# Mamba, convolution, attention and shift blocks on one Trainium2 core: the shift block moved from a common tail into the attention loops

## The chip, the cores and the metric

The kernel runs on one core of one Trainium2 chip. The metric is the device time in microseconds (us) of one execution; lower is better. Engines: TensorE (PE; its weight loads are PEld), VectorE (DVE), ScalarE (ACT), GpSimd (POOL) and SyncE (SP), which only starts DMAs.

## The reference

The input x has 16 images of 64 channels of 32x32 pixels, f32. Four residual blocks follow one another, each on the group-normalized x (32 groups of two channels):

1. x += a small Mamba block (state 2) over 1024 positions per image;
2. x += a 3x3 convolution block with batch norm and a 1x1 convolution;
3. x += attention over the 1024 positions of an image: scores from two 32-channel PReLU projections, values from a 64-channel one, softmax over all positions;
4. x += a shift block. Each channel c has a shift theta[c] = (dy, dx). The image is zero-padded, taken at the whole part ft of the shift and one pixel further, and blended with the fractional part dt:

```python
z1 = xp[:, cidx, y0[:, :, None], x0[:, None, :]]
z2 = xp[:, cidx, y0[:, :, None], x1[:, None, :]]
z3 = xp[:, cidx, y1[:, :, None], x0[:, None, :]]
z4 = xp[:, cidx, y1[:, :, None], x1[:, None, :]]
s = z1 * (1 - dy) * (1 - dx) + z2 * (1 - dy) * dx + z3 * dy * (1 - dx) + z4 * dy * dx
s = s * w_dw[None, :, None, None]
return jnp.einsum('bchw,oc->bohw', s, w_pw)
```

The shifts reach over the whole image, so a channel may see mostly padding.

## The kernel before, in words

X holds all of x in the core's memory: partition = image of the pair (2) x channel (64), then 8 pairs, then L = 1024 pixels; HALF is 512. Work goes pair by pair (p = 0 to 7). The order on each engine is written out by hand, and semaphores join them: `then_inc` at the producer, `wait_ge` at the consumer. An engine runs its own list strictly in order, so a wait holds all that is behind it.

**Blocks 1 and 2** (until about 305 us). The convolution's turns (turn1, L1634) already carry the first pair's attention operands and row products. In this stage DVE and ACT also prepare half of the hat matrices of block 4 (distance L759, hat_abs L1070, hat_relu L1075).

**Block 3, the attention loops** (attend: PE L1751, DVE L723, ACT L1180, POOL's sums L1383). Loop p has 16 slots n, one for each of two images (par) and 8 chunks j of 128 keys. In slot n:

- PE: scores(p, n), two matmuls of 512 queries (L1710); two row products of the next pair (rows, L1688), from which the softmax maxima of loop p+1 come; products (L1723), two matmuls that multiply the exponentials with the values. Extras stand in fixed slots: maxima transposed (max_rows, L1700) after slots 0 and 14, operands of pair p+2 (L1666) in slot 2, sums of pair p-1 (L1743) in slots 5 and 6, values of pair p+1 (L1677) in slots 9 and 10.
- ACT: probs, two exponentials of 128x512 (L1154), which scores of the next slot wait for (two PSUM banks); copies and PReLU parts of operands(p+2), inverse (L1176, L1178) for the softmax sum of p-1.
- DVE: two maxima (L692), which rows of the next slot wait for; operands(p+2), add_first (L721), biased, negative and positive (L670, L678, L684) for the values, scaled and residual (L709, L712) of pair p-1 in slots 7 and 8, end_stats (L456) in slots 9 and 14.
- POOL: normed(p+3) (L1368), low_z(p+2) (L1381), then sums(p): for j = 2 to 7 two adds of 128x1024 (L1391), both operands in SBUF. Four slots hold exponentials, so probs waits for adds of j-4.
- SP: stacked(q), 12 DMAs that build the stacked operands of pair q.

In the last loop (lead=False: no row products, no operands, no values) DVE makes all adds (add, L847), since POOL clears buffers for the hat matrices; block 3 of pair 6 ends in that loop, and the group statistics of pairs 0 to 5 are computed in it (coefs_stat L422, group L1467, coefs_var L431, root L1001, coefs_shift L439).

**Block 4, the common tail.** After loop 7: the sums of pair 7, its residual and statistics; all eight pairs are normalized (normed3), transposed so that image, row, or column lie on the partitions (L1840, 64 transposes, copied out by ACT L1248 and DVE L319), shifted in y and in x by 64 + 64 matmuls with hat matrices, one per channel (shift_y L1850, shift_x L1861, with copies L895 and L1261), transposed back (L1896, copies L327 and L1248), multiplied by the 1x1 weights (pointwise3, L1884), added to X (add3, L906) and stored (L410, L413). The hat matrices hold 1 - |distance| where positive, on a block diagonal of buffers cleared by POOL (L1399, L1402); half of them are placed by SP's DMAs, half by DVE and ACT (L839, L1085) in the tail.

The small steps of the statistics, on which the prediction leans (L422):

```python
link(v.tensor_tensor(SQ[:, lo:hi], mean, mean, ALU.mult))                 # L428
v.tensor_tensor(var, var, SQ[:, lo:hi], ALU.add).then_inc(s["stat_ready"], 1)   # L429
```

Of the kernel before, what the change touches and what calls it, by code (L numbers as in the profile page):

```python
# [23 lines left out]
F32 = mybir.dt.float32  # L24
F32R = mybir.dt.float32r
BF16 = mybir.dt.bfloat16
ACT = mybir.ActivationFunctionType
# [13 lines left out]
EPS = 1e-5  # L41

# [59 lines left out]
def build(nc, x, pack, out):  # L102
    with ExitStack() as ctx:
# [14 lines left out]
        EX = sb("EX", [P, 2 * L])  # L118
        MB = sb("MB", [P, 2, CHUNKS, 2], BF16)
        IB = sb("IB", [P, P], BF16)  # L120
        PS = ctx.enter_context(nc.psum_tensor("PS", [P, 8, HALF], F32))
# [60 lines left out]
        ONE = small(1)  # L182
        PRELU = small(2)
# [45 lines left out]
        def both_stacks(b):  # L229
            k = 4 * ((b + 2) % 3)  # L230
            return R[:, k * L:(k + 4) * L].rearrange("p (k e h n) -> p k e h n", k=2, e=2, h=2)
        G3 = RA
        SLOTS = 4
        PT = [[RB[:, (2 * n + par) * L:(2 * n + par + 1) * L] for par in range(2)] for n in range(SLOTS)]
        SA = [[t[:, par * L:(par + 1) * L] for par in range(2)]
              for t in (RB[:, 8 * L:10 * L], RB[:, 10 * L:12 * L], EX)]
        V = [v.rearrange("p (c m) -> p c m", c=CHUNKS)
             for v in (RA[:, 4, :], RB[:, 12 * L:13 * L], RB[:, 13 * L:14 * L])]
        GB = [RB[:, 14 * L:15 * L], RA[:, 5, :], RA[:, 6, :]]
        OT = [RA[:, 7, 0:HALF], RA[:, 7, HALF:L]]  # L240
        EQ, EF = [[RA[:, i, h * HALF:(h + 1) * HALF] for h in range(2)] for i in (0, 2)]

        ZEARLY = [R[:, i * L:(i + 1) * L] for i in (5, 6)]
        ZLATE = [WS[:, i, :] for i in range(2)]

# [23 lines left out]
        def stacks_in(n):  # L269
# [4 lines left out]
        CG = 16  # L274
        ZEROED = (4, 8, 15, 16)
        D = RB[:, 0:PAIRS * L].rearrange("p (c g) -> p c g", c=C)
        AM = [[v.rearrange("p (c m) -> p c m", c=CG) for v in vs]
              for vs in ([R[:, k * L:(k + 2) * L].bitcast(F32) for k in (4, 6)],
                         [R[:, k * L:(k + 2) * L].bitcast(F32) for k in (8, 10)],
                         [RB[:, k * L:(k + 2) * L] for k in (8, 10)],  # L280
                         [RB[:, k * L:(k + 2) * L] for k in (12, 14)])]
        D1 = [WS[:, 0, i * HALF:(i + 1) * HALF].bitcast(F32) for i in range(2)]
        HAT = [[t.rearrange("p (c y) -> p c y", c=CG)
                for t in (W[:, OFF[w]:OFF[w] + HALF], RB[:, (30 + a) * HALF:(31 + a) * HALF],
                          EX[:, a * HALF:(a + 1) * HALF], EX[:, (2 + a) * HALF:(3 + a) * HALF])]
               for a, w in enumerate(("e12", "bc0"))]
        E = RA.rearrange("p b n -> p (b n)").rearrange("p (x g c) -> p x g c", g=4, c=C)
        S3 = RB[:, 0:PAIRS * L].rearrange("p (b n) -> p b n", b=PAIRS)


# [1685 lines left out]
```

## Time and profile before

| | us |
|---|---|
| median of 3 runs | 698.72 |
| lowest and highest | 695.61, 700.11 |
| span of the profiled execution (first to last record) | 697.9 |
| PE busy | 625.1 (90% of the span) |
| DVE busy | 535.1 (77%) |
| ACT busy | 429.5 (62%) |
| POOL busy | 385.2 (55%) |
| start of loop 7, and from there to the end of the span | 589.86, 108.0 |

The profiled execution has its span as its own time here; it lies 0.8 under the median of the runs. In the rows below a time is us from the span's start; a timeline row gives start, length, engine, line, operation, out<-in with partitions x elements, and x the number of instructions merged; a bracket tells an idle time before it and what ended it. An f32 matmul leaves two records. In the rows of stretches, PEclk is the granted TensorE clock as a share of 2.4 GHz.

### The profile page before, as it was taken

The numbers are of one execution on the slowest core, as the hardware profiler recorded it, in microseconds if no ns is written. First come the engines' busy times: TensorE is split into PE (matmuls) and PEld (weight loads), VectorE is DVE, ScalarE is ACT, GpSimd is POOL, SyncE is SP. The second block draws the span as 40 slices with busy tenths as digits, with TensorE's granted clock in tenths as the row PEclk, the third lists the DMA queues.
The fourth block names the chain that finished last, engine by engine and source line by source line (L and its number), as shares of the span: only waits on it lengthen the run. The fifth ranks groups of instructions, "written<-read, shape, count | busy, mean of one in ns | idle before, by whom it ended". The sixth has DMA issues, their size and how long they took to land.

```text
span 697.9 us, 8622 instructions
## 1 busy us (share of the span) xinstructions
PE 625.1 (90%) x2812; PEld 275.6 (39%) x2812; DVE 535.1 (77%) x857; ACT 429.5 (62%) x737; POOL 385.2 (55%) x243
## 2 busy tenths in 40 slices
PE   3795888888789989999989999999999999986996
PEld 1232332233353332234434444343444444335982
DVE  6996899999934465888858787887878888685547
ACT  2478689899644331235555765748476565787772
POOL 2454788887512140216939779595968979430000
PEclk9997999999999997999989999999999999998999
DMA  9000000000015482404003040300304020200006
GB/s 328 7 0 0 1 0 0 0 0 0 1 45 140 112 199 54 106 1 91 0 1 90 1 91 0 71 21 9 83 0 91 0 31 1 30 1 0 1 1 241
DMA packets 28533, 32.36 MB, mean 46 GB/s; under 512 B 16976, under 2 KB 17104, under 8 KB 28368
## 3 DMA queue, kind: packets, MB, share of 16 engines
q1 hardware_dynamic: 27056, 27.33, 15.3%
q10 hardware_dynamic: 1440, 4.55, 2.7%
q8 instruction: 21, 0.34, 0.2%
q14 instruction: 16, 0.13, 0.1%
HBM read 5.83 MB, written 4.19 MB: 14 GB/s over the span
## 4 chain that ended last, share of the span: by engine, by line
PE 58%; DVE 19%; issue 8%; ACT 7%; POOL 4%; DMA 1%; SPq 1%; DVEq 0%; POOLq 0%; ACTq 0%
PE PS L1723 15%; PE PS L1710 10%; PE PS L1688 9%; PE PS L1599 5%; DVE RB L476 3%; PE PS L1608 2%; PE PS L1677 2%; PE PS L1743 2%; DVE RB L552 2%; DVE PS L544 2%; DVE RB L851 2%; DVE RB L559 1%; PE PS L1850 1%; DVE SM L456 1%; DVE SM L692 1%
## 5 line engine op out<-in xcount | busy, mean ns | idle before, releaser
L692 DVE TENSOR_REDUCE SM<-PS 128x1 f32<-128x512 f32 x256 | 165.0, 683 | 65.3 <-PE PS L1688 64.7
L1154 ACT ACTIVATE RB<-PS 128x512 f32<-128x512 f32 x256 | 138.9, 594 | 88.0 <-PE PS L1710 86.9
L1391 POOL TENSOR_TENSOR RB<-RB 128x1024 f32<-128x1024 f32 x60 | 141.1, 2372 | 7.1 <-DVE RB L721 4.8
L1710 PE MATMUL PS<-R 98*128 98x512 f32 x256 | 95.5, 452 | 1.3 <-ACT RB L1154 1.3
L1688 PE MATMUL PS<-R 96*128 96x512 f32 x256 | 88.7, 418 | 6.9 <-DMA R<-R 3.2
L1723 PE MATMUL PS<-RB 128*64 128x512 f32 x320 | 85.4, 616 | 0.0
L1710 PEld LDWEIGHTS PS<-R 98*128 98x128 f32 x256 | 38.8, 189 | 83.4 <-ACT RB L1154 53.9
L1526 PE MATMUL PS<-RA,W 128*128 (+1 forms) x128 | 63.1, 636 | 8.7 <-DVE RB L552 5.3
L1688 PEld LDWEIGHTS PS<-R 96*128 96x128 f32 x256 | 48.7, 193 | 43.1 <-DVE SM L692 18.9
L1391 POOL TENSOR_TENSOR EX<-EX,RB 128x1024 f32<-128x1024 f32 x24 | 56.5, 2373 | 0.8
L1723 PE MATMUL PS<-RB,RA 128*64 128x512 f32 x192 | 52.7, 627 | 0.0
L1381 POOL TENSOR_TENSOR WS<-RA,WS 128x512 fp32r<-128x512 f32 x12 | 18.7, 1562 | 51.6 <-ACT WS L1129 33.2
L1526 PEld LDWEIGHTS PS<-RA,W 128*128 128x128 f32 x128 | 24.5, 201 | 46.0 <-issue 27.5
L1599 PE MATMUL PS<-RB,WC 128*64 128x512 f32 x168 | 41.7, 613 | 0.9 <-DVE RB L640 0.9
L1091 ACT ACTIVATE RB<-X,SM 64x1024 f32<-64x1024 f32 x15 | 18.5, 1242 | 35.8 <-PE PS L1599 24.4
L552 DVE TENSOR_TENSOR_SCAN RB<-RB,PS 128x512 f32<-128x512 f32 x32 | 38.3, 1237 | 0.6
L1160 ACT ACTIVATE R<-PS 2x512 fp32r<-2x512 f32 x32 | 17.2, 582 | 27.7 <-PE PS L1700 27.7
L456 DVE BATCH_NORM_STATS2 SM<-X 128x6 f32<-128x512 f32 x48 | 31.7, 683 | 1.1 <-DMA X<-x 0.8
L476 DVE SCALAR_TENSOR_TENSOR RB<-PS,W,RB 128x1023 f32<-128x1023 f32 (+2 forms) x24 | 30.6, 1280 | 1.5 <-ACT RB L931 0.8
L1321 POOL TENSOR_TENSOR RB<-RB 128x512 f32<-128x512 f32 x16 | 20.3, 1268 | 16.1 <-ACT RB L978 16.0
L1330 POOL TENSOR_TENSOR EX<-RB 128x512 f32<-128x512 f32 x15 | 19.1, 1277 | 17.8 <-DVE RB L564 17.8
L1723 PEld LDWEIGHTS PS<-RB 128*64 128x64 f32 x320 | 16.2, 135 | 30.6 <-issue 26.5
(186 smaller groups left out, 1111.7 us busy)
## 6 DMA issues: line engine op xcount, KB each, us to landing
R<-WS SPq DMA_DIRECT2D x72, 128.0 KB, 2.4
X<-x SPq DMA_DIRECT2D x8, 512.0 KB, 7.4
RB<-RB SPq DMA_DIRECT2D x32, 128.0 KB, 4.0
RB<-RB ACTq DMA_DIRECT2D x14, 280.5 KB, 4.1
out<-X SPq DMA_DIRECT2D x7, 512.0 KB, 2.7
R<-R SPq DMA_DIRECT2D x20, 128.0 KB, 2.4
W<-pack SPq DMA_DIRECT2D x1, 1072.0 KB, 11.6
R<-R ACTq DMA_DIRECT2D x4, 128.0 KB, 3.3
```

The source lines that it names most:

```text
L456: return v.bn_stats(BST[:, p, h, :], half(X, p, h))
L476: i = v.scalar_tensor_tensor(AC[b][:, j:L], xp[:, 0:L - j], col("cw%d" % (3 - j)), AC[b][:, j:L], ALU.mult, ALU.add)
L552: i = v.tensor_tensor_scan(tB[h][j], tA[h][j], bank(1 + j), first, ALU.mult, ALU.add)
L692: v.tensor_reduce(MX[:, par, tile, h:h + 1], bank(2 + h), AX.X, ALU.max)\
L1154: act(slot[:, h * HALF:(h + 1) * HALF], bank(4 + h), ACT.Exp).then_inc(s["p_ready"], 1)
L1321: link(g.tensor_tensor(tM[h], tM[h], tU[h], ALU.add))
L1391: i = g.tensor_tensor(out, out, PT[j % SLOTS][par], ALU.add)
L1526: i = mm(bank(1 + 2 * o + j), mat("bc%d" % (2 * o + j)), half(XS, p, h))
L1599: i = mm(conv_out(k, h), WC[:, 3 * k + dx, :], u[:, y, dx:dx + WW], start=(k == 0 and dx == 0), stop=(k == 1 and dx == 2))
L1688: mm(bank(2 + h), stack(b, par, 0)[0:96, tile * P:(tile + 1) * P], stack(b, par, 1)[0:96, h * HALF:(h + 1) * HALF]).then_inc(s["s_mm"], 1)
L1710: mm(bank(4 + h), stack(b, par, 1)[0:98, j * P:(j + 1) * P], stack(b, par, 0)[0:98, h * HALF:(h + 1) * HALF]).then_inc(s["t_mm"], 1)
L1723: i = mm(PS[par * C:(par + 1) * C, h, :], V[b][:, j, par * C:(par + 1) * C], PT[j % SLOTS][par][:, h * HALF:(h + 1) * HALF], start=(j == 0 ...
```

## The change

Block 4 is no longer a tail over all pairs. Each pair's block 4 is done in the loops that follow its attention: statistics and normalization of pair p-1 in loop p, then a copy in device memory, shifted windows read back from it, blends and the 1x1 matmul in loop p+1 and p+2. There are no hat matrices, transposes and shift matmuls.

- norm3(q) (ACT) writes the normalized pair into PADDED, 32 rows with a pitch of 65, of which 32 are data. spread_out(q) (SP) writes PADDED, 1.06 MB, into one of two scratch tensors in device memory, whose pads were zeroed at the start.
- windows(q) (POOL) issues two indirect DMAs. Each takes, for each of 128 partitions, one run of 1073 elements from the scratch at an offset that depends on the channel's whole shift: 16 output rows and one more. The second takes the lower half of the image, for the other image of the pair, so that halves lie in swapped partitions.
- rows_part and cols_part (ACT) multiply by 1 - fraction, rows_blended and cols_blended (DVE) add the neighbour times the fraction, rows first, then columns; 33 rows of 33 or 32 elements.
- pointwise3 (PE), four matmuls of 64x64 weights, add3 (DVE), store (SP).
- places() and theta() (DVE) compute offsets and fractions in the convolution, in place of distance and the hat operations.
- In the attention itself the values' PReLU is done by ACT (v_parts, two operations a half) and DVE (mixed, one), not by DVE alone; operands, sums, values, high_z, inverse, scaled and residual stand one slot later; SA and V have two buffers, not three.
- In loop 7 the adds are split: DVE adds image 0, POOL image 1, and POOL issues windows(5), windows(6) and windows(7) between.

The diff, cut to its core:

```diff
@@ sync
+            sp.wait_ge(s["zero_set"], 1)
+            for t, of in zip(spread, blocks):
+                sp.dma_start(t[0:LEAD].rearrange("(p n) -> p n", p=16), R[0:16, 0:LEAD // 16].bitcast(F32))\
+                    .then_inc(s["pads_in"], 16)
+                sp.dma_start(of[:, HH * PITCH:BLOCK], R[:, 0:FAR * PITCH].bitcast(F32)).then_inc(s["pads_in"], 16)
+            def spread_out(q, parts=1):
+                need(sp, s["windows_in"], 32 * (q - 1))
+                for h in range(parts):
+                    sp.wait_ge(s["g3_dve" if h else "g3_done"], 1 if h else q + 1)
+                    r = slice(h * HH * PITCH // parts, (h + 1) * HH * PITCH // parts)
+                    sp.dma_start(blocks[q % 2][:, r], PADDED[:, r]).then_inc(s["g3_out"], 16)
...
+            for p in range(1, PAIRS - 1):
+                if p >= 3:
+                    store(p - 3)
+                if p + 2 < PAIRS:
+                    stacked(p + 2, (p + 2) % 3)
+                spread_out(p - 1)
+            store(4)
+            spread_out(6)
+            store(5)
+            spread_out(7, 2)
+            store(6)
@@ vector, attend
+                        if n == 0 and p >= 3:
+                            cols_blended(p - 3)
+                        if n == 2 and p >= 3:
+                            add3(p - 3, 6)
+                        if n in (4, 6) and p + 2 < PAIRS:
                             operands(p + 2, n // 5)
                         if n in (v0 + 1, v0 + 2):
                             biased(p + 1, n - v0 - 1)
+                        if n in (v0 + 2, v0 + 3):
+                            mixed(p + 1, (p + 1) % 2, n - v0 - 2)
...
+                        if n in (8, 9):
+                            scaled(p - 1, n - 8)
+                            residual(p - 1, n - 8)
+                        if n == 10:
+                            end_stats(p - 1, 0)
+                            link(end_stats(p - 1, 1))
+                            coefs_stat(p - 1, p)
+                        if n == 11:
+                            coefs_var(GN3 + p - 1, p - 1, p)
+                        if n == 13:
+                            coefs_shift(GN3 + p - 1, p - 1, p)
+                        if n == 14 and p >= 2:
+                            rows_blended(p - 2)
@@ vector, loop 7 and the end
+            cols_blended(4)
+            add3(4, 2)
...
+            coefs_stat(q, q + 1)
+            add(2)
+            coefs_var(GN3 + q, q, q + 1)
+            rows_blended(5)
+            add(3)
+            coefs_shift(GN3 + q, q, q + 1)
+            add(4)
+            cols_blended(5)
+            add(5)
+            add(6)
+            add3(5, 2)
+            add(7)
...
+            norm3(q, 1)
+            rows_blended(6)
+            cols_blended(6)
+            add3(6, 2)
+            for h in range(2):
+                rows_blended(q, h)
+                cols_blended(q, h)
+            add3(q, 4)
@@ scalar
+            def v_parts(q, b, c):
+                a.wait_ge(s["asm_done"], 2 * q + c + 1)
+                act(v_chunks(b, c), bank(6 + c), ACT.Identity, scale=col("aa")).then_inc(s["v_linear"], 1)
+                act(bank(6 + c), bank(6 + c), ACT.Relu).then_inc(s["v_relu"], 1)
+            def rows_part(q, h=None):
+                k = rows_of(h)
+                a.wait_ge(s["windows_in"], 32 * (q + 1))
+                need(a, s["cols_done"], 2 * q)
+                act(BLENDS[:, k], WINDOWS[:, k, 0:WIDE], ACT.Copy, scale=REST[:, 0:1])\
+                    .then_inc(s["rows_act"], 2 if h is None else 1)
...
+                    if n in (v0 + 1, v0 + 2) and lead:
+                        v_parts(p + 1, (p + 1) % 2, n - v0 - 1)
+                    if lag and lead:
+                        if n == 9 and p >= 2:
+                            rows_part(p - 2)
+                        if n == 12:
+                            root(GN3 + p - 1, p - 1, p)
+                        if n == 14:
+                            norm3(p - 1)
+                        if n == 15 and p >= 2:
+                            cols_part(p - 2)
@@ gpsimd
+            def windows(q):
+                if q == 0:
+                    g.wait_ge(s["pads_in"], 16 * 4)
+                    g.wait_ge(s["places_done"], 1)
+                g.wait_ge(s["g3_out"], 16 * (q + 1) + (16 if q == PAIRS - 1 else 0))
+                need(g, s["pw_mm"], 2 * q)
+                table = spread[q % 2].unsqueeze(1)
+                for h in range(2):
+                    at = bass.IndirectOffsetOnAxis(ap=PLACES[:, h:h + 1], axis=0)
+                    g.indirect_dma_start(SEEN[:, h * WINDOW:h * WINDOW + WINDOW - WW], None, table, at)\
+                        .then_inc(s["windows_in"], 16)
...
+                if p >= 2:
+                    windows(p - 2)
...
+                sums(p)
+            p = PAIRS - 1
+            windows(p - 2)
+            g.wait_ge(s["first_added"], 2 * PAIRS)
+            for j in range(2, 6):
+                add(p, j, 1, True)
+            windows(p - 1)
+            for j in range(6, CHUNKS):
+                add(p, j, 1, True)
+            windows(p)
@@ tensor
     def operands_free(q):
                     t.wait_ge(s["m_copied"], 4 * q - 4)
+                    need(t, s["res_done"], 2 * q - 8)
...
+                    if n == 1 and p >= 3:
+                        if lead:
+                            t.wait_ge(s["m_copied"], 4 * p + 4)
+                            pointwise3(p - 3, 6)
+                        else:
+                            t.wait_ge(s["s_read"], 32 * PAIRS)
+                            pointwise3(p - 3, 2)
...
+                    v0 = 8 if first else 10
+                    if n == v0 and lag and lead:
+                        t.wait_ge(s["x2_done"], 2 * p)
+                        group(GN3 + p - 1, p - 1, p)
                     if n in (v0, v0 + 1) and lead:
+                        if lag and n > v0:
+                            t.wait_ge(s["var_ready"], GN3 + p)
                         values(p + 1, (b + 1) % 3, n - v0)
```

## Rows read from the trace of the kernel before

**Rows 1.** Busy time by stretch: stretch, length, busy us of each engine, PEclk, DMA, GB/s
```profile
500.00:550.00 50.00, 50.00 (x220) 21.49 (x220) 42.31 (x75) 31.62 (x59) 41.01 (x19) 1.00 0.14 32
```

**Rows 2.** Timeline of PE: a slot of loop 5, what follows it, the starts of loops 6 and 7
```profile
510.57 0.74 PE L1710 MATMUL PS<-R 98*128 98x512 f32 x2
...
511.71 1.08 PE L1723 MATMUL PS<-RB 128*64 128x512 f32 x4
...
512.72 0.61 PE L1700 MATMUL PS<-IB,MB 128*2 128x128 bf16 x8
...
550.70 0.74 PE L1710 MATMUL PS<-R 98*128 98x512 f32 x2
...
589.86 0.73 PE L1710 MATMUL PS<-R 98*128 98x512 f32 x2
```

**Rows 3.** Timeline of PE in loop 7 and the tail: group(), next scores, pointwise3, next entry
```profile
595.62 0.39 PE L1472 MATMUL PS<-SM,W 128*128 128x12 f32 x2
...
595.86 0.70 PE L1710 MATMUL PS<-R 98*128 98x512 f32 x2
...
680.62 1.09 PE L1884 MATMUL PS<-RB,W 64*64 64x512 f32 x8 [0.31 <-DVE RB L327]
...
681.64 1.09 PE L1896 MATMUL PS<-W,RA 128*128 128x128 f32 x8
```

**Rows 4.** Timeline of DVE, loop 5: add_first, maxima, scaled, end_stats
```profile
522.88 1.21 DVE L721 TENSOR_TENSOR EX<-RB 128x1024 f32<-128x1024 f32 x1
...
529.82 1.29 DVE L692 TENSOR_REDUCE SM<-PS 128x1 f32<-128x512 f32 x2 [1.17 <-PE PS L1688]
...
531.02 0.69 DVE L709 TENSOR_TENSOR PS<-PS,RA 128x512 f32<-128x512 f32 x1
...
536.08 0.68 DVE L456 BATCH_NORM_STATS2 SM<-X 128x6 f32<-128x512 f32 x1
```

**Rows 5.** Timelines of DVE and POOL: the statistics' small steps, two adds, the steps undisturbed
```profile
591.20 1.10 DVE L428 TENSOR_TENSOR SM<-SM 128x6 f32<-128x6 f32 x1
...
592.34 2.30 DVE L429 TENSOR_TENSOR SM<-SM 128x6 f32<-128x6 f32 x1
...
589.91 4.71 POOL L1391 TENSOR_TENSOR RB<-RB 128x1024 f32<-128x1024 f32 x2 [0.31 <-ACT RB L1154]
...
632.17 0.16 DVE L429 TENSOR_TENSOR SM<-SM 128x2 f32<-128x2 f32 x1
```

**Rows 6.** Timeline of POOL in loop 5: the adds behind low_z
```profile
528.54 16.75 POOL L1391 TENSOR_TENSOR EX<-EX,RB 128x1024 f32<-128x1024 f32 x7
```

**Rows 7.** Timeline of ACT: a pair of exponentials, root, normed3 of 1024 columns
```profile
529.34 1.09 ACT L1154 ACTIVATE RB<-PS 128x512 f32<-128x512 f32 x2 [0.65 <-PE PS L1710]
...
634.34 0.21 ACT L1005 ACTIVATE SM<-SM 128x2 f32<-128x2 f32 x1
...
635.54 1.20 ACT L1235 ACTIVATE RA<-X,SM 128x1024 f32<-128x1024 f32 x1
```

**Rows 8.** Timeline of PE and stretches in the convolution: a wait and the clock around it
```profile
259.80 1.22 PE L1688 MATMUL PS<-R 96*128 96x512 f32 x2 [3.17 <-DMA R<-R]
...
250.00:256.00 6.00, 6.00 (x36) 2.78 (x36) 4.02 (x6) 1.98 (x2) 4.69 (x4) 1.00 0.86 210
...
259.80:262.00 2.20, 2.20 (x10) 0.80 (x10) 1.29 (x2) 0.00 (x0) 0.00 (x0) 0.50 1.01 220
```

**Rows 9.** Timelines of PE and DVE in the tail: sums of pair 7, last add3
```profile
624.97 1.94 PE L1743 MATMUL PS<-RB,W 128*64 128x512 f32 x8 [1.85 <-DVE RB L851]
...
689.53 5.01 DVE L906 TENSOR_TENSOR X<-PS,X 128x512 f32<-128x512 f32 x8 [0.16 <-PE PS L1884]
```

**Rows 10.** DMA issues of the page (KB, us to landing), and SP's last two stores
```profile
X<-x SPq DMA_DIRECT2D x8, 512.0 KB, 7.4
...
out<-X SPq DMA_DIRECT2D x7, 512.0 KB, 2.7
...
693.97 1.11 SPq L413 DMA_DIRECT2D out<-X  x2
```

More of the change, by code:

```diff
@@ L182, in build @@
         ONE = small(1)
+        OMAA = small(1)
+        THETA = small(2)
+        WHOLE = small(2)
+        ABOVE = small(2)
+        FRAC = small(2)
+        REST = small(2)
+        OFFSET = small(1)
+        OFFSETX = small(1)
+        START = small(1)
         PRELU = small(2)
@@ L787, in _ @@
                 biased(0, c)
-                negative(0, 0, c)
-                positive(0, 0, c)
-            at = 0
+            for c in range(2):
+                mixed(0, 0, c)
             for p in (5, 6, 7):
@@ L1219, in _ @@
                     low_stacked()
+                    for c in range(2):
+                        v_parts(0, 0, c)
             max_rows(0, 0, 0)
@@ L1232, in _ @@
-            attend(PAIRS - 1, 1, lead=False, extra=late)
-            def normed3(p):
-                act(G3[:, p, :], X[:, p, :], ACT.Identity, scale=SC[:, p:p + 1], bias=SH[:, p:p + 1])\
-                    .then_inc(s["g3_act"], 1)
-            a.wait_ge(s["coef_ready"], GN3A + 1)
-            for p in range(2, PAIRS - 2):
-                normed3(p)
+            q = PAIRS - 2
+            attend(PAIRS - 1, 1, lead=False,
+                   extra={6: lambda: inverse(q, 0), 7: lambda: inverse(q, 1), 8: lambda: rows_part(5),
+                          10: lambda: root(GN3 + q, q, q + 1), 11: lambda: cols_part(5), 13: lambda: norm3(q)})
@@ L1241, in _ @@
+            q = PAIRS - 1
             for h in range(2):
[L1242 removed]
+                product_out(q, h)
             for h in range(2):
[L1244 to L1258 removed]
@@ L1272, in _ @@
+            root(GN3 + q, q, PAIRS)
+            norm3(q, 0)
+            rows_part(6)
+            cols_part(6)
+            for h in range(2):
+                rows_part(q, h)
+            for h in range(2):
+                cols_part(q, h)
         @block.gpsimd
@@ L1359, in g1 @@
                     .then_inc(s["g1_ready"], 1)
-            for p in range(5):
+            for p in range(3):
+                g1(p)
+            g.memset(PADDED[:, :], 0.0).then_inc(s["pads_set"], 1)
+            for p in (3, 4):
                 g1(p)
@@ L1903, in _ @@
-            t.wait_ge(s["bk_act"], 8)
-            t.wait_ge(s["bk_dve"], 8)
-            for p in range(4, PAIRS):
-                pointwise3(p)
+                sums(PAIRS - 1, h)
+            t.wait_ge(s["x2_done"], 2 * PAIRS)
+            group(GN3 + PAIRS - 1, PAIRS - 1, PAIRS)
+            t.wait_ge(s["res_done"], 2 * 5 + 2)
+            pointwise3(6, 2)
+            t.wait_ge(s["p_ready"], 32 * PAIRS)
+            pointwise3(7, 4)
 def _packed(w):
```

510 lines of the change are left out of this document (176 added, 334 removed).

## The prediction

> **What bounds the kernel now.** I read the busy time by stretch first: from 500 to 550 us PE is busy all 50 us, DVE 42, POOL 41 and ACT 32 [rows 1]. The attention loops are bound by PE. The timeline of PE says how: one slot n of a loop is scores and two row products, 1.14 us until products() begins, and products(), 1.01 until the next entry, so 2.15 us [rows 2]. Sixteen slots and the extras (maxima, z operands, sums, values) give the period: loop 6 starts at 550.70, loop 5 started at 510.57, so 40.1 us; loop 7 starts at 589.86 [rows 2]. From there to the span's end at 697.9 lie 108.0 us: loop 7 and the tail, where all pairs are transposed, shifted by hat matrices and turned back.
>
> So the question has two halves: what the new work adds to loops 1 to 6, where each us of PE or of PE's waiting is paid, and what is left after 589.86. I write T10 for the start of slot 10, and so on.
>
> **Part 1, PE work added to the loops.** pointwise3 is four matmuls in four quadrants, 1.02 us to the next entry [rows 3], in loops 3 to 6: 4.1. group() is 0.25 [rows 3], in loops 1 to 6: 1.5. Moving operands, sums and values by a slot costs PE nothing.
>
> **Part 2, the wait at group().** PE meets group() in slot 10, at T10 + 2.15, and it waits for stat_ready. DVE makes that in its own slot 10, behind the two maxima of slot 10. A maximum pair begins 1.02 after its slot and takes 1.20, scaled with residual 1.35 per half, two end_stats 1.25 [rows 4, 2]. From T8: maxima until +2.2, scaled and residual until +3.6, maxima until +4.8, scaled and residual until +6.1, maxima until +7.3, end_stats until +8.6, bn_aggr until +8.8. T10 is +4.3, so DVE reaches the two tiny tensor_tensors at T10 + 4.55. Undisturbed they take 0.16 each [rows 5], and PE would wait 3.0.
>
> They are disturbed. Both read two SBUF operands, and POOL is in its adds. At the end of loop 6 the same two lines took 1.10 and 2.30, and they end at 592.30 and 594.64, where POOL's two adds, which start at 589.91 and take 4.71, end too [rows 5]. So the first waits for the add that runs, and the second for the whole next add (2.37, [rows 6]). In loops 1 to 5 POOL begins its adds after low_z: high_z moves from slot 5 to slot 6, so 2.15 later than T5 + 5.7 (528.54, [rows 6]), at T5 + 8.0, that is with j=3's second add still running when DVE arrives at T5 + 17.0. I price the rest of that add at 0.4, the whole next one at 2.37: the wait is 3.0 + 0.1 + 0.4 + 2.4 = 5.9. Its bounds are 3.0 and 3.0 + 2.4 + 2.4 = 7.8. In loop 6, without low_z, the adds start earlier and POOL runs dry after the fourth j: 4.45. The Trainium skill, page "SBUF — State Buffer", section on who interferes with whom, says that a VectorE instruction with two SBUF inputs and a GpSimd instruction that reads SBUF exclude each other for a whole instruction. By that rule the wait is the 5.9; by the undisturbed rows it would be 3.0, and that is the second case below.
>
> **Part 3, waits behind it.** In slot 11 values(1) waits for var_ready: maxima until T11 + 2.2, biased (0.7, as scaled) until 2.9, three small ops of 0.2 and a step to PE make 3.6 against 2.15: 1.45. In slot 12 ACT's v_parts waits for biased (T12 + 2.95), takes 1.3, root takes 0.46 [rows 7], and only then comes the exp of slot 13 (half of 1.09, [rows 7]), which scores of slot 14 needs: ready at T12 + 5.4 and 5.9 against 4.3: 1.35 with its second half. At the loop's end coefs_shift (two SBUF operands) and rows_blended meet adds of POOL again, up to 2.37 each; ACT's norm3 stands behind the first, in front of the copies of maxima and the last exps. Walked through, the next loop's scores and rows come 1.8 late (0.9 in loop 1, which has no rows_blended). cols_blended (1.3, as an add of 1024 columns, 1.21, [rows 4]) is blocked until an add ends, and pointwise3 waits for it: 0.8 in loops 3 to 6. operands_free waits for res_done: maxima of slot 2 and two add3 end at T2 + 3.6, PE is there at 2.75: 0.9 in loops 3 to 5. Bounds of this whole part: 0, if DVE and ACT were ahead, and twice my sum, as an add blocks each time fully.
>
> Per loop: p=1: 5.9 + 0.25 + 1.45 + 1.35 + 0.9 = 9.85. p=2: 10.75. p=3, 4, 5: 10.75 + 1.0 + 0.8 + 0.9 = 13.45 each. p=6: 4.45 + 0.25 + 1.45 + 1.35 + 1.8 + 1.8 = 11.1. Together 72.0.
>
> **The clock.** After a wait of 3.17 us at 259.80 PE ran at 0.50 of its clock, the 1.2 GHz level, against 1.00, the 2.4 GHz level, before [rows 8]; eight matmuls took twice as long. A wait of 5.9 in each loop can do that. The slow stretch then lies over slots 11 to 13, where PE waits anyway (1.45 and 1.35), so most is absorbed: 0.5 a loop, 3.0 in all (bounds 0 and 4 a loop).
>
> **Part 4, loop 7 and the tail, from T0 = 0.** POOL's window issue and its wait are new rows. Before, DVE made all adds of loop 7 and the sums stood at 624.97, 35.1 after 589.86 [rows 9, 2]. Now half of them are POOL's, and ACT carries probs (1.09 a slot), inverse (1.2 a half), rows_part, cols_part and norm3 (1.23 for 1024 columns, [rows 7]). Walked through: a slot of PE is 1.7 without row products; pointwise3(4) adds 1.0; probs(3) ends at 8.1; sums(6) stand at 9.7 and 12.2; inverse ends at 13.4 and 15.9, rows_part(5) at 18.3; DVE's residual(6) at 17.3, its statistics at 19.9 (POOL waits for probs then, so one add at most is in the way); group at 20.8, root at 22.4; rows_blended(5) is held by an add and ends at 24.9, so cols_part(5) at 26.2 and probs(11) at 27.3; coefs_shift is held until 28.5, and norm3(6) ends at 29.9. spread_out(6) writes 1.06 MB; a store of 512 KB lands in 2.7 [rows 10], so two in a row would take 5.4; I take 4.3 and 0.7 to issue: 35. POOL stands in windows(6) for it, with adds j=6 and 7 behind: two issues at 0.9 (SP's are 0.56; upper bound a whole landing, 7.4, [rows 10]), then 4.75 for adds: sums at 42.1 with the steps between. From the sums to coef_ready it was 10.0 (624.97, [rows 9]; root ended at 634.8, [rows 7], and coefs_shift follows), of which root stood 0.7 behind copies: 9.3, so 51.4. norm3(7): 52.0. Meanwhile pair 6 is blended (four steps of 1.3 and pointwise3, to 58.4), and windows(7) needs pw_mm of pair 6, so spread_out(7), there at 57, is hidden. windows(7): 1.8 to issue, 2.7 to land (bounds 2.7 and 7.4, [rows 10]): 63. Blends by halves: rows, rows, columns, columns, across ACT and DVE, 5.1; pointwise3 1.0, add3 1.4, with steps 70.7. From the last DVE op (689.53 + 5.01) to the end 3.4 [rows 9]: 74.1, against 108.0. The Trainium skill, page "DMA: Bandwidth & Descriptors", section on the anatomy of one DMA, gives some 2.0 us plus bytes over 436 GB/s for a DMA issued by GpSimd, 3.3 for 549 KB (an estimate from it): with it the tail would be 0.6 longer. No row here shows such a DMA.
>
> **What goes or is hidden.** Removed are 64 + 64 transposes, 128 shift matmuls, their copies and POOL's clears: all in the 108.0. In the convolution ACT loses eight hat operations, DVE four distances and gains some 20 small ones; PE is the bound there; 0, bounds -3 and +4. The pads are written long before their use. In loops 2 to 6 windows() stands before low_z, where POOL waits for high_z; that hides it until an issue costs over 4 us.
>
> **Sum.** 589.9 + 72.0 + 3.0 + 74.1 = 739.0 of span; the span before, 697.9, is 0.8 under the median of its runs, 698.7, so 740.
>
> **Rivals.**
> B, *the adds don't meet the statistics*: PE waits 3.0 at group, the clock stays, the loop boundary is smooth: 740 - 16 (5 x 2.9 and 1.45) - 3 (clock) - 8 (the boundary's 9.9 but 1.9) = 713. For it: a shift of half a us decides on which add DVE falls. Against: [rows 5], the same lines.
> C, *the waits of PE vanish*: DVE has 8 us free in 50, and if the statistics come before PE asks, only PE's work is added: 589.9 + 5.6 + 74.1 + 0.8 = 670, faster. It decides where PE waits less than (108.0 - 74.1 - 5.6) / 6 = 4.7 us a loop. Against: slot 10 stands in both queues, and 2.2 of the wait remain with DVE on time.
> D, *the indirect DMAs are dear*: at 5 us of POOL for each, four stand on the tail's path: 740 + 4 x 4.1 = 756. Nothing in the trace speaks for or against.
> E, *it doesn't do what it says*: windows move in 4-byte pieces, 128 x 1073 of them twice a pair, 275,000: far above 1000.
>
> **Chances.** A 0.5, B 0.2, C 0.05, D 0.15, E 0.02; 0.08 lies between B and C, about no change. Predicted 740; the range takes in B and D with their bounds: 704 to 764. This kernel's measurement tells about 1% from no change. Faster by over 1% (under 691.7): 0.06; within: 0.08; slower: 0.86.
>
> **What would show it.** Right: PE waits for the two-operand statistics line once a loop, some 6 us; loops 3 to 5 last 53 to 54; the granted clock dips after it; tensor_tensor of 128x1 shows over 1 us; from loop 7 to the end some 75. Wrong: loops of 42 to 46 (C), or of 47 to 50 with those lines at 0.16 (B); POOL's issue over 3 us (D).

## The result, and the profile after

The changed kernel takes 730.2 us (median of 4 runs, 729.7 to 732.5) against 697.7 for the kernel before, run beside it: ratio 1.046, interval 1.042 to 1.050. Predicted were 740 with a range of 704 to 764. The direction held, and so did the ground of it, that PE waits in the loops for more than the tail gives back. The largest single term, the wait at group(), came out at half its size. The total was 10 us too high, and two errors of opposite sign hide in that: the loops came out 14.5 us shorter than forecast, the tail 6 us longer. (The profiled execution is the slowest of the four, 2.3 us over their median.)

The page of the changed kernel, busy time of the engines, and then its busy time by stretch in the same 50 us as [rows 1]:

```profile
span 730.6 us, 7908 instructions
...
PE 606.2 (83%) x2440; PEld 240.0 (33%) x2440; DVE 540.0 (74%) x854; ACT 422.1 (58%) x734; POOL 399.1 (55%) x250
```

```profile
500.00:550.00 50.00, 44.19 (x174) 18.30 (x173) 37.93 (x60) 30.62 (x56) 32.48 (x17) 0.93 0.30 86
```

PE was busy all 50 us and is now busy 44, at 0.93 of its clock: the loops aren't bound by PE any more. No other engine has taken over as a whole (DVE 38, POOL 32); what bounds them is a chain that passes back and forth. Who PE waits for stands in its waits in loops 1 to 6 (line waited at, releaser, total, times, longest):

```profile
PE PS L1501 <- DVE SM L451: 18.5, 6, 3.6
PE PS L1740 <- ACT RB L1197: 5.0, 11, 0.7
PE PS L1785 <- DVE RB L749: 2.8, 4, 0.7
PE PS L1718 <- DVE X L756: 2.6, 3, 0.9
...
PE PS L1707 <- DVE SM L458: 1.4, 3, 0.8
```

L1501 is group(), waiting for the statistics; L1740 are the scores, which wait for exponentials; L1785 is pointwise3, behind cols_blended; L1718 is the row product behind operands_free. L1707 are the second values, which wait for var_ready. All five are waits that the prediction named, but not in its sizes: the largest is 3.0 a loop, not 5.9, and the second values wait 1.4 in six loops together, not 1.45 in each. PE's timeline of slots 10 and 11 of loop 3 shows it, and what it does to the clock:

```profile
475.17 1.08 PE L1753 MATMUL PS<-RB,W 128*64 128x512 f32 x4
479.23 0.35 PE L1501 MATMUL PS<-SM,W 128*128 128x2 f32 x2 [2.98 <-DVE SM L451]
479.44 1.14 PE L1707 MATMUL PS<-W,RA 128*128 128x128 f32 x8
480.33 1.00 PE L1740 MATMUL PS<-R 98*128 98x512 f32 x2
481.13 1.05 PE L1718 MATMUL PS<-R 96*128 96x512 f32 x2
482.12 1.98 PE L1753 MATMUL PS<-RB,W 128*64 128x512 f32 x4
```

The same products() take 1.08 ahead of the wait and 1.98 behind it: 2.4 GHz, then 1.2. DVE in that time, and POOL's run of adds:

```profile
478.59 0.29 DVE L450 TENSOR_TENSOR SM<-SM 128x1 f32<-128x1 f32 x1
478.92 0.16 DVE L451 TENSOR_TENSOR SM<-SM 128x1 f32<-128x1 f32 x1
...
491.22 1.83 DVE L466 SCALAR_TENSOR_TENSOR SM<-SM 128x1 f32<-128x1 f32 x1
...
494.28 2.23 DVE L742 SCALAR_TENSOR_TENSOR RA<-RB,SM,RA 128x1089 f32<-128x1089 f32 x1
...
499.51 3.00 DVE L749 SCALAR_TENSOR_TENSOR RB<-RA,SM,RB 128x1056 f32<-128x1056 f32 x1
```

```profile
469.39 19.02 POOL L1423 TENSOR_TENSOR RB<-RB 128x1024 f32<-128x1024 f32 x8
```

The two small statistics steps of [rows 5], there 1.10 and 2.30, are nearly free here (L450, L451). But coefs_shift (L466) on one element takes 1.83, and the two blends (L742, L749) 2.23 and 3.00. The adds did meet DVE: not at group(), but at the loop's end, where Part 3 of the prediction has them too.

The starts of slot 0 (by the maxima product of each loop) give loops 1 to 6 as 52.9, 49.3, 50.9, 52.2, 51.6 and 49.6 us, against 45.4, then 40.1 four times and 38.7: 62.0 us more in all. (Two other profiles with the same instructions in these loops, experiments 8 and 9, have 304.8 and 302.7 us in place of 306.6, so this sum is good to some 4 us.) The scores of loop 7 start at 650.39 ([rows 2]: 589.86), and 80.2 us follow, against 108.0. PE, POOL and ACT in the tail:

```profile
692.58 3.42 PE L1773 MATMUL PS<-RB,W 128*64 128x512 f32 x8 [2.43 <-POOL RB L1423]
700.91 0.56 PE L1501 MATMUL PS<-SM,W 128*128 128x2 f32 x2 [4.91 <-DVE SM L451]
708.99 1.98 PE L1785 MATMUL PS<-RB,W 64*64 64x512 f32 x8 [7.52 <-DVE RB L749]
724.81 1.99 PE L1785 MATMUL PS<-RB,W 64*64 64x512 f32 x8 [13.83 <-DVE RB L749]
```

```profile
711.81 0.95 POOL L1438 DMA_INDIRECT RB<-spread,PLACES  x1 [19.28 <-PE PS L1785]
713.07 0.94 POOL L1438 DMA_INDIRECT RB<-spread,PLACES  x1 [0.30 <-issue]
...
719.36 1.38 ACT L1151 ACTIVATE RA<-RB,SM 128x528 f32<-128x528 f32 x2 [11.94 <-DMA RB<-spread,PLACES]
```

The sums of pair 7 stand behind POOL's last adds (start 42.2 after loop 7's start; predicted 42.1), then POOL stands idle 19.28 us until the pointwise product of pair 6 lets it issue the windows of pair 7. ACT stands idle 11.94 us until these have landed; 7.55 of them lie behind the first issue.

### The profile page after: what moved, and what is told of

It reads as the page before. It is cut to its first block, busy times and chain, and to the rows that moved or that the text cites. A ratio compares the mean times of both kernels' runs of the same rounds, so it can differ in the third digit from the quotient of the medians.

```text
span 730.6 us, 7908 instructions
## 1 busy us (share of the span) xinstructions
PE 606.2 (83%) x2440; PEld 240.0 (33%) x2440; DVE 540.0 (74%) x854; ACT 422.1 (58%) x734; POOL 399.1 (55%) x250
## 4 chain that ended last, share of the span: by engine, by line
DVE 37%; PE 34%; issue 11%; POOL 6%; ACT 6%; DMA 3%; SPq 1%; DVEq 0%; POOLq 0%; ACTq 0%
DVE SM L707 10%; PE PS L1740 5%; PE PS L1718 5%; PE PS L1753 4%; PE PS L1628 4%; DVE RB L498 3%; PE PS L1707 3%; POOL RB L1423 3%; DVE SM L478 2%; PE PS L1637 2%; DVE RB L749 2%; PE PS L1773 2%; DVE RB L575 2%; DVE SM L466 2%; DVE PS L567 2%
## 5 line engine op out<-in xcount | busy, mean ns | idle before, releaser
L1423 POOL TENSOR_TENSOR RB<-RB 128x1024 f32<-128x1024 f32 x90 | 213.7, 2393 | 52.3 <-ACT RB L1197 43.5
L1740 PE MATMUL PS<-R 98*128 98x512 f32 x256 | 101.3, 468 | 8.1 <-ACT RB L1197 7.9
L1718 PE MATMUL PS<-R 96*128 96x512 f32 x256 | 94.6, 435 | 10.3 <-DVE X L756 2.6
L1740 PEld LDWEIGHTS PS<-R 98*128 98x128 f32 x256 | 41.2, 194 | 95.2 <-ACT RB L1197 65.1
L1753 PE MATMUL PS<-RB,RA 128*64 128x512 f32 x256 | 71.8, 641 | 0.0
L1753 PE MATMUL PS<-RB,W 128*64 128x512 f32 x256 | 71.2, 641 | 0.0
L1718 PEld LDWEIGHTS PS<-R 96*128 96x128 f32 x256 | 49.6, 197 | 52.3 <-DVE SM L707 24.9
L1418 POOL TENSOR_TENSOR WS<-RA,WS 128x512 fp32r<-128x512 f32 x12 | 15.3, 1276 | 65.9 <-ACT WS L1138 54.0
L1501 PE MATMUL PS<-SM,W 128*128 128x2 f32 (+3 forms) x28 | 6.4, 300 | 35.1 <-DVE SM L451 34.6
L1438 POOL DMA_INDIRECT RB<-spread,PLACES x16 | 15.5, 970 | 35.0 <-PE PS L1785 27.6
L1785 PE MATMUL PS<-RB,W 64*64 64x512 f32 x64 | 10.5, 729 | 24.1 <-DVE RB L749 24.1
```

What stands on the lines that cost most here:

```text
L1423: i = g.tensor_tensor(SA[p % 2][par], SA[p % 2][par], PT[j % SLOTS][par], ALU.add)
L1718: mm(bank(2 + h), stack(b, par, 0)[0:96, tile * P:(tile + 1) * P], stack(b, par, 1)[0:96, h * HALF:(h + 1) * HALF]).then_inc(s["s_mm"], 1)
L1740: mm(bank(4 + h), stack(b, par, 1)[0:98, j * P:(j + 1) * P], stack(b, par, 0)[0:98, h * HALF:(h + 1) * HALF]).then_inc(s["t_mm"], 1)
L1753: i = mm(PS[par * C:(par + 1) * C, h, :], V[p % 2][:, j, par * C:(par + 1) * C], PT[j % SLOTS][par][:, h * HALF:(h + 1) * HALF], start=(j ...
```

## The experiments

Line numbers in an experiment's rows are its own; the operations are named beside them. Unless it says otherwise, an edit is to the changed kernel, and it is printed without the parts that only carry it ("..."). T1 and T2 are the theories of each expectation. The expectations name a run by a label: e4 and e5 are experiments 4 and 5, e6 is 8, e8 and e10 stand in 10. The medians of the kernel before, run beside each experiment, lie between 697.0 and 699.8, so totals from different experiments compare to some 3 us. The same stretches, loops 1 to 6 in sum, serve for all: 244.6 us before, 306.6 after the change.

**1. group() without its wait.**

```
 def group(nth, lo=0, hi=PAIRS):
+    if GN3 <= nth < GN3 + PAIRS - 2:
+        mm(PS[:, 7, 0:2], mat("pairs"), FIXED).then_inc(s["group_mm"], 1)
+        return
     t.wait_ge(s["stat_ready"], nth + 1)
```

> In loops 1 to 6 the group product reads two constants and no longer waits for the statistics (they are still made). Its result in those loops is that of the constants, so the per-pair coefficients differ. Theory T1 (the 3.0 us wait at the group product sits in TensorE's path and nothing is behind it but a shorter wait at the second part of the values): each loop loses 3.0 us of wait and some 0.3 us of half clock, while about 1.2 us of wait stays at the second values; loops 49.3 to 52.9 become 46 to 49.5, total 708 to 713 us. Rival T2 (VectorE bounds the stretch, so the wait only moves): the second values wait 4 us or more in its place and the total stays above 724 us.

Measured: 708.7 us, loops 287.3, 19.3 less. PE's waits in these loops:

```profile
PE PS L1712 <- DVE SM L459: 12.1, 6, 2.5
```

The wait at the second values is now 2.0 a loop, more than the 1.2 of the expectation. T1 holds: the wait, with the half clock behind it, is worth 3.2 us a loop, although part of it comes back one slot later.

**2. GpSimd busy, but not reading.**

The three memsets stand in for the add in loops 1 to 6 alone:

```
-    i = g.tensor_tensor(SA[p % 2][par], SA[p % 2][par], PT[j % SLOTS][par], ALU.add)
+    link(g.memset(SA[p % 2][par], 1.0))
+    link(g.memset(SA[p % 2][par], 1.0))
+    i = g.memset(SA[p % 2][par][:, 0:128], 1.0)
```

> In loops 1 to 6 each of GpSimd's adds of probabilities is three memsets of about the same time in all (the sums of probabilities are then constants): GpSimd is as busy and signals as late, but reads nothing from SBUF. Theory T1 (GpSimd's two-operand adds hold up VectorE's instructions with two SBUF operands): the coefs_shift step falls from 1.83 to under 0.3 us, the rows blend from 2.23 to about 1.35, the cols blend from 3.00 to about 1.35, and the loops get 1 to 2.5 us shorter each: 715 to 724 us. Rival T2 (it is GpSimd being busy, or its writes): durations and total as they are, 728 to 732 us. The group wait stays at 3.0 us in both.

Measured: 716.5 us, loops 291.8, 14.8 less. DVE's timeline at the end of loop 3 (coefs_shift, rows blend, cols blend):

```profile
486.28 0.15 DVE L466 SCALAR_TENSOR_TENSOR SM<-SM 128x1 f32<-128x1 f32 x1
...
487.67 1.35 DVE L742 SCALAR_TENSOR_TENSOR RA<-RB,SM,RA 128x1089 f32<-128x1089 f32 x1
...
492.41 1.31 DVE L749 SCALAR_TENSOR_TENSOR RB<-RA,SM,RB 128x1056 f32<-128x1056 f32 x1
```

T1: 1.83 became 0.15, 2.23 became 1.35, 3.00 became 1.31. A set of memsets takes some 2.2 us, not 2.37, so GpSimd's run ends a little sooner; the durations of DVE's own rows don't depend on that. PE's wait at group() stays, 17.0 us in six loops. Without the two-operand adds each loop is 2.5 us shorter; how much of that is owed to the sooner end isn't separated.

**3. GpSimd's run shifted.**

```
     if j == 2:
         g.wait_ge(s["first_added"], 2 * p + 2)
+        if p:
+            for k in range(2):
+                g.memset(W[:, OFF["dtl"]:OFF["ones"]], 0.0)
+                g.memset(W[:, OFF["winx"]:OFF["winx"] + 2 * P], 0.0)
+                link(g.memset(mat("w11"), 0.0))
```

> In loops 1 to 6 GpSimd clears two unused stretches for about 2.4 us before its run of adds, so that the boundary at which VectorE's small steps after the statistics fall is no longer between two sums but within one, where the next add follows with no wait of GpSimd between. Theory T1 (the predicted 2.4 us at that place were missing only because the boundary fell between two sums, where GpSimd waits on itself and VectorE gets in twice): the square step or the add behind it takes 2 us or more in most loops and the group wait goes from 3.0 to 4.5 to 5.9 us; total 738 to 748 us. Rival T2 (small steps aren't held up at such a boundary): group wait 2.9 to 3.3 us, total 728 to 733 us.

Measured: 740.6 us, loops 318.1, 11.5 more; group() waits 28.9 us in six loops, 4.8 each. The timelines of DVE in loops 3 and 6 and of POOL in the same two:

```profile
477.94 2.05 DVE L450 TENSOR_TENSOR SM<-SM 128x1 f32<-128x1 f32 x1
480.02 0.16 DVE L451 TENSOR_TENSOR SM<-SM 128x1 f32<-128x1 f32 x1
...
637.20 0.45 DVE L450 TENSOR_TENSOR SM<-SM 128x1 f32<-128x1 f32 x1
637.69 2.26 DVE L451 TENSOR_TENSOR SM<-SM 128x1 f32<-128x1 f32 x1
```

```profile
470.54 18.94 POOL L1423 TENSOR_TENSOR RB<-RB 128x1024 f32<-128x1024 f32 x8
...
625.72 14.21 POOL L1423 TENSOR_TENSOR RB<-RB 128x1024 f32<-128x1024 f32 x6
```

An add is 2.37. POOL adds in pairs, one add for each image of the same j, and behind each pair it waits for its own semaphore. In loop 3 the first step waits out the fourth add (ends 470.54 + 4 x 2.37 = 480.0), the second of a pair, and the second step slips in. In loop 6 the first step gets in at the end of the fifth add (637.6), within a pair, where the sixth add follows at once; the second step then takes 2.26, as in [rows 5].

The edit did its aim in loop 6 alone. In loops 1 to 5 the boundary is still the one between two pairs (second step 0.16 each time), and the wait grew from 3.0 to some 4.7 only because the first step met the fourth add earlier: 2.04 to 2.07 in place of 0.29. The total lies in T1's range, but the 28.9 us are not the 34 that the prediction had charged, and for the most part not of its kind. What the traces bear out is narrower than T1. Twice a step came behind one that had just got in within a pair, and it took a whole add (2.30 in [rows 5], 2.26 here). Between two pairs, in loops 1 to 5 of this run and of the changed kernel, it took 0.16 each time. That POOL's wait for its semaphore is what lets it in is read from the code; no run takes that wait away.

**4. Ask one slot later.** Values first part in slot 10, group() in slot 11, values second part in slot 12; the other engines follow.

```
-    if n == v0 and lag and lead:            # PE: group
+    if n == v0 + 1 and lag and lead:
...
-    if n in (v0, v0 + 1) and lead:          # PE: values
+    if n in (v0, v0 + (2 if lag else 1)) and lead:
...
+    if lag and n == 12:                     # DVE, ahead of the maxima
+        coefs_var(GN3 + p - 1, p - 1, p)
```

> In loops 1 to 6 the order of TensorE is: values first part in slot 10 as now, group product in slot 11, values second part in slot 12; VectorE makes the variance at the start of slot 12, the bias and mix of the second part one slot later each, and ScalarE's second part likewise. Nothing is left out. Theory T1 (the waits of slots 10 to 13 come only from asking for a result of VectorE one slot too early): group wait under 0.5 us, no wait at the values, 4 to 5.5 us less per loop: 697 to 706 us. Rival T2 (VectorE's own work bounds slots 8 to 15, so each wait comes back one slot later or at the maxima rows): less than 2 us per loop, 718 to 728 us.

Measured: 712.3 us, loops 286.8. Between the two theories: 19.8 us less, 3.3 a loop. The wait at group() is gone (0.6 us once in six loops), but the maxima product has one that wasn't there. PE's waits at it, and its timeline at the end of loop 3:

```profile
PE PS L1730 <- DVE RA L699: 9.6, 3, 3.2
PE PS L1730 <- DVE W L699: 8.1, 3, 3.2
```

```profile
483.96 0.61 PE L1730 MATMUL PS<-IB,MB 128*2 128x128 bf16 x8 [3.17 <-DVE RA L699]
...
485.63 1.78 PE L1753 MATMUL PS<-RB,W 128*64 128x512 f32 x4
```

The mix of the second values, now in slot 14 behind two maxima and behind coefs_shift (2.07 us beside an add), is late for the maxima product, which takes over its bank.

**5. The same, with the second bias and mix ahead of the maxima** of slots 13 and 14, and the shift made by ScalarE.

```
+    if lag and lead and n == v0 + 3:        # DVE, ahead of the maxima
+        biased(p + 1, 1)
+    if lag and lead and n == v0 + 4:
+        mixed(p + 1, (p + 1) % 2, 1)
...
+    act(SH[:, p - 1:p], GS[:, p - 1, 0:1], ACT.Copy, scale=SC[:, p - 1:p])   # GS holds the negated mean
```

> The order of e4, and in loops 1 to 6 the second part's bias and mix stand ahead of the maxima of slots 13 and 14, and the shift (the mean times the root) is made by ScalarE behind its own root, so that VectorE no longer has the small step that took 2.07 us beside GpSimd's adds. Nothing is left out. Theory T1 (in e4 the 3.2 us wait of the maxima rows came from the late second mix and the held-up small step): that wait falls under 0.5 us, 2.5 to 3.3 us less per loop than e4, total 692 to 699 us. Rival T2 (VectorE is the bound of the stretch with its maxima, bias, mix and blends): the wait comes back at the maxima or at the operands of the next loop, and the total stays at 705 to 712 us.

Measured: 684.9 us, under the 692 to 699 of T1 and below the kernel before: ratio 0.981 (0.978 to 0.985). Loops 45.1, 41.2, 43.7 three times, 42.3, in sum 259.7: with all the new work in them they cost 15 us more than before, not 62. Busy time in the stretch of [rows 1], and all waits of PE in the loops:

```profile
500.00:550.00 50.00, 48.63 (x216) 20.66 (x216) 43.60 (x77) 35.46 (x64) 40.59 (x20) 1.00 0.36 102
```

```profile
PE PS L1727 <- DVE X L760: 2.6, 3, 0.9
PE PS L1727 <- POOL RB L1414: 2.3, 1, 2.3
PE PS L1794 <- DVE RB L753: 1.6, 4, 0.4
PE PS L1739 <- DVE MB L722: 1.0, 1, 1.0
PE PS L1510 <- DVE SM L451: 0.6, 1, 0.6
```

The clock is 1.00 and PE the bound again. (The wait of 2.3 for POOL stands in the kernel before as well.) 27 us lie between this kernel and experiment 4, more than the 17.7 of the waits removed; the clock behind them, 1.78 for 1.08 in experiment 4's rows, is part of it.

**6. Which of experiment 5's two edits was it?** Experiment 5 with the shift back on VectorE:

> e5 with the shift back on VectorE, behind the four small steps of slot 13, as after the change. Nothing is left out. e4 stood at 712, e5 at 685 us. Theory T1 (the one small step held up by GpSimd's adds, 1.8 to 2.1 us on VectorE, stands in the path): 1.5 to 3 us per loop come back, 693 to 703 us. Rival T2 (VectorE has the slack for it once the bias and mix stand ahead of the maxima): within 3 us of e5, 683 to 688 us.

Measured: 683.8 us. T2: no difference. The small step still stands beside the adds, but takes 0.43 us where it falls now, and the mix behind it has slack:

```profile
468.85 0.43 DVE L470 SCALAR_TENSOR_TENSOR SM<-SM 128x1 f32<-128x1 f32 x1
469.32 0.75 DVE L703 SCALAR_TENSOR_TENSOR RA<-PS,SM,RA 128x512 f32<-128x512 f32 x1
```

So moving bias and mix ahead in DVE's queue made the difference, with no help from ScalarE. It also moved the small step to where an add is nearly over (0.43 to 0.45 in loops 1 to 5); what a step held up for 2 us would cost in this order, no run shows.

**7. The clock.** In PE's wait before group():

```
+    for k in range(46):
+        mm(PS[:, 6, (k % 4) * P:(k % 4 + 1) * P], IB[:, :], IB[:, :])
```

> Loops 1 to 6 get 46 small products of TensorE (128 columns each, results unused) in the 3.0 us wait before the group product; nothing else differs. Theory T1 (the half clock behind the wait costs 0.3 to 1 us per loop, partly inside waits that follow anyway): the scores and the products of slot 11 run at full clock (0.73 and 1.08 us in place of 1.00 and 1.98), and the total falls by 0 to 4 us: 726 to 730 us. Rival T2 (the clock makes up much of what the loop lost): 6 us or more less, under 724 us. Rival T3 (the fill delays the group product itself): more than 731 us.

Measured: 721.4 us, 8.8 less, and loops 297.4, 9.2 less. My own theory T1 (0 to 4) is too low, T2 holds. (Against the profiles of experiments 8 and 9 the loops are 7.4 and 5.3 less; the medians of the runs are what the 8.8 rests on.) The granted clock of loops 2 to 6 is 1.00 each, for 0.93 to 0.97, and products() of slot 11 takes 1.08 again. The wait at the second values, 7.2 us in six loops here, was hardly there after the change (1.4):

```profile
PE PS L1707 <- DVE SM L458: 7.2, 6, 1.2
```

At half clock PE came to it later; that much was absorbed, as predicted. But some 9 us net, 1.5 a loop, were not.

**8. The tail.** Pair 7's windows in a buffer of their own, pair 6's issued behind POOL's last adds:

```
-    need(g, s["pw_mm"], 2 * q)
+    if q == PAIRS - 1:
+        g.wait_ge(s["pv_done"], 2 * CHUNKS * PAIRS)
+        g.wait_ge(s["add_dve"], 6)
...
-    for j in range(2, 6): add(p, j, 1, True)
-    windows(p - 1)
-    for j in range(6, CHUNKS): add(p, j, 1, True)
+    for j in range(2, CHUNKS): add(p, j, 1, True)
+    windows(p - 1)
     windows(p)
```

(The last lines are set in short form.)

> Only loop 7 and the tail differ from the kernel after the change: the windows of pair 7 go to a buffer of their own and wait for the spread copy instead of the pointwise product of pair 6, and GpSimd issues the windows of pair 6 behind its last two adds. Nothing is left out. Theory T1 (both waits are on the path that ends last): the sums start 3 to 5 us earlier, the windows of pair 7 are issued about 5 us earlier against coef_ready, total 720 to 724 us. Rival T2 (another chain takes over: the stores, or the blends of pair 6 on ScalarE and VectorE, which then stand between the landing and the blends of pair 7): the total falls by less than 3 us, 727 us or more.

Measured: 723.3 us. From loop 7's maxima product to the end 71.6 us against 78.0. PE's sums and the two pointwise products, and POOL's issue for pair 7:

```profile
687.56 1.94 PE L1786 MATMUL PS<-RB,W 128*64 128x512 f32 x8
...
703.07 1.99 PE L1798 MATMUL PS<-RB,W 64*64 64x512 f32 x8 [7.53 <-DVE RB L760]
715.64 1.99 PE L1798 MATMUL PS<-RB,W 64*64 64x512 f32 x8 [10.59 <-DVE RB L760]
...
701.93 1.80 POOL L1453 DMA_INDIRECT RB<-spread,PLACES  x1 [12.39 <-DMA spread<-EX]
```

The total lies in T1's range, but of its two parts the sums start 2.3 us earlier, not 3 to 5 (37.7 against 39.9 behind loop 7's maxima product); the issue comes 4.0 earlier against coef_ready, for 5. The issue now waits for the spread copy, and comes 1.1 us before pair 6's pointwise product instead of 2.8 behind its start.

**9. Is the gather dear?** Plain copies from a fixed place for pair 7 in place of indirect ones:

```
...
+    src = blocks[q % 2][:, h * (HH // 2) * PITCH:h * (HH // 2) * PITCH + WINDOW - WW]
+    g.dma_start(SEEN[:, h * WINDOW:h * WINDOW + WINDOW - WW], src).then_inc(s["windows_in"], 16)
```

> Only the two windows of pair 7 differ from the kernel after the change: plain copies from a fixed place of the scratch (the zero shift's), issued by GpSimd at the same point, in place of indirect ones. Where the true places are other ones the last pair's output differs. Theory T1 (the 6.2 us from issue to landing are the bytes of two windows, 1.1 MB, one behind the other): the landing stays at 5 to 7 us and the end moves by less than 1.5 us. Rival T2 (gathering by a table of places costs its own time, on GpSimd or in the queue): landing under 4 us and the end 2 us or more earlier.

One run, 726.7 us; its loops 4 to 6, in which nothing differs, were 1.2 to 1.4 us shorter than in the other profile, so the total says nothing here. The issues and ScalarE's wait do, and the median of the landings:

```profile
706.09 1.14 POOL L1439 DMA_DIRECT2D RB<-spread  x2 [18.20 <-PE PS L1790]
...
713.54 1.38 ACT L1151 ACTIVATE RA<-RB,SM 128x528 f32<-128x528 f32 x2 [11.67 <-DMA RB<-spread]
...
RB<-spread POOLq DMA_DIRECT2D x2, 536.5 KB, 5.9
```

7.45 us from the first issue to the blends, against 719.36 - 711.81 = 7.55 for the indirect pair. T1, as far as the gather goes: it isn't what makes the landing long. That it is the size alone is not shown, since the size wasn't varied, and there is a rival that the traces do show. In the changed kernel a store of 512 KB leaves at about the same time as the windows, of every pair but pair 0. Pair 0's two windows, with no store beside them, land in 5.0 us (median of the two), the others in 5.7 to 6.3. So some 1 us of the 6.3 seems to go with the store; no run takes it away.

**10. Both repairs, and two more steps.** Experiments 5 and 8 together:

> e5 and e6 together; nothing is left out. If both act on different stretches, the gains add: e5's total less what e6 took off 730, 684 to 692 us, below the kernel before. Rival: the tail's gain vanishes when the loops are shorter, 692 to 699 us.

Measured: 677.8 us, ratio 0.973 (0.969 to 0.976): better than the 684 to 692 expected, since experiment 5 itself was.

> e8 with small products of TensorE whose results aren't used (76, 108 and 150 of them) in its three waits of the tail. Nothing is left out. Theory T1 (the half clock of the tail lengthens only what TensorE does behind those waits): the two pointwise products take 1.0 in place of 1.98 us and the last group product 0.35 in place of 0.56, of which the half before the first sum counts: 1 to 2.5 us off the total, 675 to 677 us. Rival T2: nothing measurable, since half of each product lies beside VectorE's adds: 677 to 679 us.

Measured: 676.9 us (676.2 to 682.0). The products behind the waits went from 1.98 to 1.09 and 1.72, the profiled spans from 674.8 to 674.0. 0.9 us between medians is within the noise: undecided, and small at best.

> e10, and the blends of pair 7 start on each window's own landing, row and column parts alternating, and in loops 3 to 5 the add of the pointwise product stands ahead of the maxima of slot 2. Nothing is left out. Expected: the first half's blends lie before the second landing (2 to 2.5 us less) and the 0.87 us waits at the operands go (up to 2.6 us in all): 670 to 674 us. If the halves' chain already ended on the second landing alone, or the add delays the maxima as much as it saves: 675 us or more.

Measured: 674.2 us, ratio 0.965 (0.962 to 0.969), the lowest median here, at the edge of the 670 to 674 expected; its interval overlaps that of the step before (0.966 to 0.976), so the step by itself isn't shown by the totals. The profiles do show both parts. Loops 3 to 5 are 42.6 in place of 43.7, and the first half's blend starts on its own landing, 4.1 us ahead of the second, and 4.9 behind its issue at 650.67:

```profile
655.52 0.75 ACT L1171 ACTIVATE RA<-RB,SM 128x528 f32<-128x528 f32 x1 [5.68 <-DMA RB<-spread,PLACES]
...
659.60 0.75 ACT L1171 ACTIVATE RA<-RB,SM 128x528 f32<-128x528 f32 x1 [1.78 <-DMA RB<-spread,PLACES]
```

## Why the prediction was right, and where it was off

The total and the direction came out, and part of that is luck. Of the prediction's five signs of being right one held, the dip of the clock. PE waited 3.0 at the statistics and not some 6, loops 3 to 5 lasted 50.9 to 52.2 and not 53 to 54, the small steps took 0.29 and 0.16 and not over 1, and the end came 80.2 behind loop 7's start and not some 75. At group() it was rival B's picture that came true. Added up over six loops, the waits forecast at group(), at the second values and at the scores were some 27 us too dear (15.3, 7.3 and 4.4); the half clock gave some 12 back (an estimate: 9.2 and 5.8 of experiment 7, less the 3 forecast), and the tail 6.

- *PE work*: as read: group() 0.21 to the next entry for 0.25, pointwise3 1.02.
- *Part 2, the wait at group()*: the 3.0 of ordering is exact (2.96 to 2.98 in loops 1 to 5, 3.60 in loop 6). The term that failed is the "2.4" for the whole next add. The first step did wait out the running add (0.29), but I took the next one for granted and didn't ask which boundary DVE would meet. It fell between two pairs of adds, where POOL waits for itself; in [rows 5] it fell within a pair. Experiment 3 brought the other boundary, and with it the whole next add, back in one loop of six. -2.9 in five loops and -0.85 in the last, 15 us: this alone is more than the whole miss of the loops.
- *Part 3*: the wait at the second values, 1.45 a loop in the forecast, was 1.4 in all; experiment 7 shows it at 1.2 a loop when PE keeps its clock. The scores' wait was 0.7 at most, not 1.35. The boundary (1.9 in loop 3, from the slots' starts), pointwise3 (0.7) and operands_free (0.9) came as worked out, 1.8, 0.8 and 0.9.
- *The clock*: 0.5 a loop was mis-sized, 1.5 measured (experiment 7). The absorption happened, at one wait of 1.2 us; the stretch at half clock cost more than that.
- *Part 4*: the start of norm3(6) and the sums' 42.1 against 42.2 after loop 7's start held to a few tenths, though the sums then took 3.4 at half clock for 1.94. coef_ready came at 52.3 for 51.4. The windows of pair 7 were the mis-sized term: "2.7 to land" was the row of one store of 512 KB, while here two windows are on their way together, with a store of pair 6 beside them: 7.55 from the first issue to the blends against 1.8 + 2.7. That is 3 us of the 6 by which the tail was longer. The other 3 lie ahead of the issue, at 61.4 behind loop 7's start for 58.4: 0.9 from coef_ready, 1.0 from pointwise3 of pair 6 at half clock (1.98), the rest in the steps between.
- *Rivals*: B (713) had the right small steps at 0.16, but not the smooth boundary nor the kept clock; the truth lay between it and the forecast. C fell as the kernel stands, but experiment 5 shows that it was an order of instructions away: all its added time, 2.5 us a loop, lies under the point from which C decides, and with the same tail it is faster than before. D fell, 0.95 us an issue; E too.

Of the loops' 62 us, 47 go with experiment 5's order, so they were waits and what hung on them, and 15 stay: 1.3 of group(), 4.1 of pointwise3, 2.6 and 1.6 of waits at the operands and pointwise3, 1.6 of two single waits; some 4 I can't assign.

## What to carry to other kernels

Work moved off the end into a loop that one engine fills costs, beyond that engine's own share, what it makes the engine wait, not what it takes: the same added instructions cost 62 us here in one order and 15 in another. Let the bound engine ask for a result one step later than the slot in which it is made, and put whatever frees a buffer for it ahead of work that only keeps pace. When a wait is repaired, look at the next slot before believing the gain: experiment 4 took 18 us of waits away at one place and found 17.7 at the next.

## What was not expected of the hardware

- A small two-operand step of VectorE that waits beside a run of GpSimd's adds gets in when the running add ends, at either kind of boundary (coefs_shift, 1.83 us, within a pair). The step right behind it gets in too where GpSimd's own semaphore wait stands at that boundary (0.16 us), and waits out a whole add where none does (2.30 in [rows 5], 2.26 in experiment 3). Among the steps of the statistics these two are the only cases of the second kind in all the traces. The Trainium skill, page "SBUF — State Buffer", on who interferes with whom, has the exclusion for whole instructions, and only against a GpSimd instruction that reads SBUF; the runs agree with both (2.05 and 2.26 against an add's 2.37; 0.15 beside memsets, experiment 2).
- A 3 us wait cost PE 1.5 us net a loop through its clock, and 46 small products inside the wait took that away (experiment 7).
- Two indirect copies of 549 KB landed as fast as two plain ones: 7.55 and 7.45 us from the first issue to the first use (experiment 9, one run).
